# A per-subject residual matmul on one core: where the store is issued, how two engines share the copies, and a new start-up

## The chip, the cores and the metric

One core of one Trainium2 chip runs the kernel. The metric is the device time of one execution in microseconds (us). Three runs of the kernel before gave 332.45, 332.52 and 333.44 us; the median is 332.52 us.

## What is computed

```python
# x (128, 128, 1024) f32, itok_B_0_7 (128,) int32 in 0..7, L0_cond_weights (8, 128, 128) f32
w = weights[subjects]                       # one 128x128 matrix for each of the 128 samples
out = jnp.einsum('bct,bcd->bdt', x, w)
return x + out
```

Each of the 128 samples is 128 channels by 1024 time steps in f32 (512 KB). It is read once and written once: 67 MB in, 67 MB out.

## The kernel before

The residual is folded into the weights: `add_eye` adds the identity to each of the eight matrices, so that a product with `w + 1` is already the output.

**Tiles and pairs.** A tile is two samples (`a` = 0, 1), each on one half of the partitions: channel `h*2 + r` of sample `a` lies on partition `a*64 + h`, in row `r`. There are 64 tiles. Two tiles make a pair (four samples, 2 MB), and there are 32 pairs; loads and stores move a whole pair. `x_ring` has 10 slots (5 pairs), `results` has places for 6 pairs, and `product` in PSUM is double buffered by tile (`PRODUCTS = 2`).

**Engines.** Each one runs a program written out by hand, and semaphores alone set the order between them:

- SP (`sync`) loads the weights and then pair after pair (L108). For the first lap it issues four loads at once, and the fifth when pair 0 has landed. A later load waits for `picked` (L105), that is until POOL has filled the weight slots of the same pair.
- POOL builds the identity. Then, for each sample, it copies the subject's matrix from `weight_bank` to `weight_ring` (L136), four copies a pair. From pair 5 on it waits until the pair that held the slots has been multiplied.
- The weight bank itself is a reordered copy of the weights in four quarters, made by the helper `bank`: two quarters on DVE (L149), two on ACT (L180). POOL waits for all four.
- PE multiplies a tile in 8 matmuls (L217), which the trace records as 16, when the copies of the tile two before are out of PSUM (`dve_copied`, `act_copied`, one initial count of `PRODUCTS` each) and, at a pair's first tile, when the pair has landed (`x_in`). Before the first tile it waits for `picked` to reach 2.
- ACT and DVE copy the product out of PSUM into `results`. A tile has 8 blocks of 32 x 1024; `ACT_BLOCKS` says how many of them, from the front, ACT takes, and DVE takes the rest:

```python
BLOCKS = [(a, q) for a in range(2) for q in range(Q)]
ACT_BLOCKS = (4, 5)
for a, q in BLOCKS[:ACT_BLOCKS[tile % 2]]:
    last = act.copy(target(tile, a, q), rows(tile, a, q))
```

- ACT also issues the store of each pair (L202), behind its last copy of the pair's second tile, once both `act_copied` and `dve_copied` count that tile. Before the first copy into a place of `results` both engines wait for the store of six pairs earlier (`pair_out`).

Of the kernel before, what the change touches and what calls it, by code (L numbers as in the profile page):

```python
# [5 lines left out]
PSUM_BANK_COLS = 512  # L6
DMA_INC = 16
SLOTS = 10
PAIR = 2
LOADS_AHEAD = 4  # L10
PRODUCTS = 2
RESULTS = 6


def subject_residual_kernel(nc, x, subjects, weights, out):
# [12 lines left out]
    S, _, D = weights.shape  # L28
# [6 lines left out]
    PAIRS, PAIR_SLOTS = TILES // PAIR, SLOTS // PAIR  # L35
# [3 lines left out]
    SUBJECT_ROWS = 16  # L39

    BLOCKS = [(a, q) for a in range(2) for q in range(Q)]
    ACT_BLOCKS = (4, 5)

    LOW, HIGH = slice(0, H), slice(H, C)
    EVENS, ODDS = slice(0, S, 2), slice(1, S, 2)
# [3 lines left out]
    out_of_pair = out.rearrange("(n g) (k q) t -> n (g k) (q t)", g=PAIR * 2, q=Q)  # L49

    with ExitStack() as ctx:
        x_ring = ctx.enter_context(nc.sbuf_tensor("x_ring", [C, SLOTS, R, T], f32))
        results = ctx.enter_context(nc.sbuf_tensor("results", [C, RESULTS, Q, T], f32))
# [8 lines left out]
        product = [[ctx.enter_context(nc.psum_tensor(f"product{i}_{a}", [D, T], f32)) for a in range(2)]  # L62
                   for i in range(PRODUCTS)]

        subjects_in = ctx.enter_context(nc.semaphore("subjects_in"))
        clamped = ctx.enter_context(nc.semaphore("clamped"))
        weights_in = ctx.enter_context(nc.semaphore("weights_in"))
# [4 lines left out]
        bank_high = ctx.enter_context(nc.semaphore("bank_high"))  # L72
# [14 lines left out]
        def target(tile, a, q):  # L87

            pair, j = divmod(tile, PAIR)
            g = j * 2 + a  # L90
            return results[g * K:(g + 1) * K, pair % RESULTS, q, :]

        def rows(tile, a, q):

            return product[tile % PRODUCTS][a][q * K:(q + 1) * K, :]
# [14 lines left out]
        @block.gpsimd  # L110
        def _(pool):
            def subjects_of(pair):

                _, numbers = nc.values_load_multi_w_load_instructions(  # L114
                    subject_row[0:1, pair * PAIR * 2:(pair + 2) * PAIR * 2], engines=(mybir.EngineType.Pool,), min_val=0,
                    max_val=S - 1, skip_runtime_bounds_check_because="DVE has clamped subject_row to 0 .. S - 1")
                return numbers

            pool.memset(eye[:, :], 0.0).then_inc(eye_zero, 1)  # L119
            pool.wait_ge(eye_zero, 1)  # L120
            for half in (LOW, HIGH):
                pool.affine_select(eye[half, :], eye[half, :], pattern=[[-1, H]], base=0, channel_multiplier=1,  # L122
                                   compare_op=mybir.AluOpType.not_equal, fill=1.0).then_inc(eye_made, 1)
            pool.wait_ge(clamped, 1)
            for pair in range(PAIRS):
                if pair % 2 == 0:
                    numbers = subjects_of(pair)
                if pair == 0:
                    pool.wait_ge(bank_low, 1)
                    pool.wait_ge(bank_high, 1)  # L130
                elif pair >= PAIR_SLOTS:
                    pool.wait_ge(multiplied, (pair - PAIR_SLOTS + 1) * PAIR)
                for j in range(PAIR):
                    slot = pair * PAIR % SLOTS + j
                    for a, half in enumerate((LOW, HIGH)):
                        done = pool.tensor_copy(weight_ring[half, slot, :, :],  # L136
                                                weight_bank[half, bass.ds(numbers[(pair % 2 * PAIR + j) * 2 + a], 1), :, :])
                    done.then_inc(picked, 1)

        @block.vector  # L140
        def _(dve):
            def add_eye(r):
                cells = weight_halves[:, :, r, slice(r, D, R)]
                return dve.tensor_tensor(cells, cells, eye[:, :].rearrange("h (s k) -> h s k", s=1).broadcast_to(  # L144
                    (C, S // 2, H)), add)

            def bank(half, source, subjects_of):

                return dve.tensor_copy(  # L149
                    weight_bank[half, subjects_of, :, :].rearrange("h i r (q k) -> h i r q k", q=Q),  # L150
                    weight_halves[source, :, :, :].rearrange("h i r (k q) -> h i r q k", q=Q))

            dve.sem_inc(dve_copied, PRODUCTS)
            dve.wait_ge(subjects_in, DMA_INC)
            dve.tensor_scalar(subject_row[0:1, :], subject_row[0:1, :], 0, S - 1, mybir.AluOpType.max,  # L155
                              mybir.AluOpType.min).then_inc(clamped, 1)
            dve.wait_ge(weights_in, DMA_INC)
            dve.wait_ge(eye_made, 2)
            add_eye(0)
            add_eye(1).then_inc(eyes_added, 1)  # L160
            dve.wait_ge(eyes_added, 1)
            bank(LOW, LOW, EVENS)
            bank(LOW, HIGH, ODDS).then_inc(bank_low, 1)
            for tile in range(TILES):
                pair = tile // PAIR
                dve.wait_ge(multiplied, tile + 1)
                if tile % PAIR == 0 and pair >= RESULTS:
                    dve.wait_ge(pair_out[pair % RESULTS], pair // RESULTS * DMA_INC)
                if tile + PRODUCTS < SLOTS:


                    dve.wait_ge(picked, tile + (PRODUCTS + 1))
                for a, q in BLOCKS[ACT_BLOCKS[tile % 2]:]:
                    last = dve.tensor_copy(target(tile, a, q), rows(tile, a, q))  # L174
                last.then_inc(dve_copied, 1)

        @block.scalar
        def _(act):
            def bank(half, source, subjects_of):
                return act.copy(  # L180
                    weight_bank[half, subjects_of, :, :].rearrange("h i r (q k) -> h i r q k", q=Q),
                    weight_halves[source, :, :, :].rearrange("h i r (k q) -> h i r q k", q=Q))

            act.dma_start(subject_row[:, :], subjects.rearrange("(one b) -> one b", one=1).broadcast_to(
                (SUBJECT_ROWS, B))).then_inc(subjects_in, DMA_INC)
            act.sem_inc(act_copied, PRODUCTS)
            act.wait_ge(eyes_added, 1)
            bank(HIGH, LOW, EVENS)
            bank(HIGH, HIGH, ODDS).then_inc(bank_high, 1)
            for tile in range(TILES):  # L190
                pair, j = divmod(tile, PAIR)
                place = pair % RESULTS
                act.wait_ge(multiplied, tile + 1)
                if j == 0 and pair >= RESULTS:
                    act.wait_ge(pair_out[place], pair // RESULTS * DMA_INC)  # L195
                for a, q in BLOCKS[:ACT_BLOCKS[tile % 2]]:
                    last = act.copy(target(tile, a, q), rows(tile, a, q))  # L197
                last.then_inc(act_copied, 1)
                if j == PAIR - 1:
                    act.wait_ge(act_copied, tile + (PRODUCTS + 1))  # L200
                    act.wait_ge(dve_copied, tile + (PRODUCTS + 1))
                    act.dma_start(out_of_pair[pair], results[:, place, :, :]).then_inc(pair_out[place], DMA_INC)  # L202
            for place in range(RESULTS):
                act.wait_ge(pair_out[place], DMA_INC * len(range(place, PAIRS, RESULTS)))

        @block.tensor
        def _(pe):
            def multiply(tile, slot, landed):
                pe.wait_ge(dve_copied, tile + 1)
                pe.wait_ge(act_copied, tile + 1)  # L210
                if slot % PAIR == 0:
                    pe.wait_ge(x_in[slot // PAIR], landed)
                for n in range(BANKS):
                    cols = slice(n * PSUM_BANK_COLS, (n + 1) * PSUM_BANK_COLS)
                    for r in range(R):
                        for a, half in enumerate((LOW, HIGH)):
                            last = pe.matmul(product[slot % PRODUCTS][a][:, cols], weight_ring[half, slot, r, :],  # L217
                                             x_ring[half, slot, r, cols], start=r == 0, stop=r == R - 1,
                                             tile_position=(a * H, 0))
                last.then_inc(multiplied, 1)  # L220

            pe.wait_ge(picked, PRODUCTS)
            with pe.Fori(0, LAPS) as lap:
                for slot in range(SLOTS):
                    multiply(lap * SLOTS + slot, slot, lap * DMA_INC + DMA_INC)
            for slot in range(REST):
                multiply(LAPS * SLOTS + slot, slot, DMA_INC * (LAPS + 1))
# [14 lines left out]
```

## Time and profile before

| What | Value |
|---|---|
| Median of three runs | 332.52 us |
| The profiled execution's own time | 333.19 us |
| Its span, first to last instruction | 331.4 us |
| ACT busy | 294.2 us, 89% |
| DVE busy | 276.7 us, 84% |
| PE busy | 238.9 us, 72% |
| Moved by DMA | 134.84 MB, mean 407 GB/s over the span |

The span is what the rows of the trace add up to. The profiled execution took 1.8 us more than its span, and 0.7 us more than the median of the three runs. A difference of 0.3% (1.0 us) is about what a measurement of this kernel can tell from no change. PE, PEld (weight loads), DVE, ACT and POOL are the engines; SPq and ACTq are the queues on which SP and ACT issue transfers.

### The profile page before, as it was taken

To read this page: it belongs to the slowest core of one execution; us is meant where nothing else is said; L and a number is where in the kernel's file an instruction comes from. 1 tells how busy PE (TensorE), PEld (TensorE's weight loads), DVE (VectorE), ACT (ScalarE), POOL (GpSimd) and SP (SyncE) were. 2 spreads that over 40 slices of the span, in tenths; PEclk is the share of its full clock that TensorE was granted. 3 is DMA by queue.
4 is the path that set the end of the run, shared out by engine and by line. 5 is a ranking of instruction groups with operands and counts; after the bars stand their busy time and mean duration, and the time that the engine had idled before them with its cause. 6 is when DMAs were issued, how large, how long until landed. Compare 5 with 4: busy or idle time off the path is not lost.

```text
span 331.4 us, 3183 instructions
## 1 busy us (share of the span) xinstructions
PE 238.9 (72%) x1024; PEld 106.1 (32%) x1024; DVE 276.7 (84%) x229; ACT 294.2 (89%) x291; POOL 51.9 (16%) x135
## 2 busy tenths in 40 slices
PE   0588787788778777877777787778778877877740
PEld 0233333334333333433343333333333433333320
DVE  3089998889988888898888889888888988888890
ACT  4189999999999999999999999999999999999991
POOL 0641011111110111111011111101111110000000
PEclk9999999999999999999999999999999999999995
DMA  7999999999999999999999999999999999996565
GB/s 285 423 421 430 424 422 430 436 427 422 435 428 434 419 428 431 430 429 437 414 428 431 440 419 435 417 441 414 431 436 420 430 433 421 439 422 279 221 255 253
DMA packets 13881, 134.84 MB, mean 407 GB/s; under 512 B 1056, under 2 KB 1584, under 8 KB 1584
## 3 DMA queue, kind: packets, MB, share of 16 engines
q1 hardware_dynamic: 9232, 67.64, 48.7%
q10 hardware_dynamic: 4640, 67.12, 47.4%
q8 instruction: 2, 0.03, 0.1%
q14 instruction: 7, 0.06, 0.0%
HBM read 67.64 MB, written 67.11 MB: 407 GB/s over the span
## 4 chain that ended last, share of the span: by engine, by line
ACT 80%; issue 11%; ACTq 3%; PE 2%; DMA 1%; POOLq 0%; DVE 0%; POOL 0%
ACT results L197 79%; ACTq L202 3%; PE product L217 2%; DMA weight_halves<-weights 1%; ACT weight_bank L180 1%; DVE weight_halves L144 0%; POOL weight_ring L136 0%; ACTq L195 0%; POOLq L114 0%; POOLq L136 0%; POOLq L130 0%
## 5 line engine op out<-in xcount | busy, mean ns | idle before, releaser
L197 ACT COPY results<-product 32x1024 f32<-32x1024 f32 x288 | 288.9, 1003 | 25.8 <-ACT results L197 14.2
L174 DVE COPY results<-product 32x1024 f32<-32x1024 f32 x224 | 273.7, 1222 | 41.0 <-PE product L217 28.2
L217 PE MATMUL product<-x_ring,weight_ring 64*128 64x512 f32 x1024 | 238.9, 605 | 80.0 <-ACT results L197 47.1
L217 PEld LDWEIGHTS product<-x_ring,weight_ring 64*128 64x128 f32 x1024 | 106.1, 188 | 211.9 <-issue 169.1
L136 POOL COPY weight_ring<-weight_bank 64x256 f32 x128 | 51.1, 399 | 220.0 <-PE product L217 206.9
L180 ACT COPY weight_bank<-weight_halves 64x1024 f32<-64x1024 f32 x2 | 4.0, 1996 | 3.3 <-DVE weight_halves L144 3.2
L155 DVE TENSOR_SCALAR subject_row<-subject_row 1x128 int32<-1x128 int32 x1 | 0.2, 214 | 3.9 <-DMA subject_row<-subjects 3.9
L180 ACT ACT_TABLE_LOAD x1 | 1.3, 1283 | 1.3 <-PEq L234 1.3
L149 DVE COPY weight_bank<-weight_halves 64x1024 f32<-64x1024 f32 x2 | 2.1, 1060 | 0.0
L144 DVE TENSOR_TENSOR weight_halves<-weight_halves,eye 128x256 f32<-128x256 f32 x2 | 0.8, 424 | 0.9 <-DMA weight_halves<-weights 0.9
L122 POOL TENSOR_SCALAR_AFFINE_SELECT eye<-eye 64x64 f32<-64x64 f32 x2 | 0.5, 236 | 0.3 <-POOL eye L119 0.2
L119 POOL MEMSET eye<- 128x64 f32 x1 | 0.2, 152 | 0.3 <-POOLq L234 0.3
L234 POOL MEMSET const-float32-0.0<- 128x1 f32 x1 | 0.1, 99 | 0.2 <-issue 0.2
L234 POOL MEMSET const-float32-1.0<- 128x1 f32 x1 | 0.1, 99 | 0.0
L234 POOL MEMSET const-bfloat16-1.0<- 128x1 bf16 x1 | 0.1, 99 | 0.0
L234 POOL MEMSET const-uint8-127<- 128x1 uint8 x1 | 0.1, 99 | 0.0
## 6 DMA issues: line engine op xcount, KB each, us to landing
x_ring<-x SPq DMA_DIRECT2D x32, 2048.0 KB, 24.3
out<-results ACTq DMA_DIRECT2D x32, 2048.0 KB, 11.7
weight_halves<-weights SPq DMA_DIRECT2D x1, 512.0 KB, 4.3
subject_row<-subjects ACTq DMA_DIRECT2D x1, 8.0 KB, 3.2
```

Of the source, the lines that this page charges most:

```text
L119: pool.memset(eye[:, :], 0.0).then_inc(eye_zero, 1)
L122: pool.affine_select(eye[half, :], eye[half, :], pattern=[[-1, H]], base=0, channel_multiplier=1, compare_op=mybir.AluOpType.not_equal, fi ...
L136: done = pool.tensor_copy(weight_ring[half, slot, :, :], weight_bank[half, bass.ds(numbers[(pair % 2 * PAIR + j) * 2 + a], 1), :, :])
L144: return dve.tensor_tensor(cells, cells, eye[:, :].rearrange("h (s k) -> h s k", s=1).broadcast_to((C, S // 2, H)), add)
L149: return dve.tensor_copy(weight_bank[half, subjects_of, :, :].rearrange("h i r (q k) -> h i r q k", q=Q), weight_halves[source, :, :, :].r ...
L155: dve.tensor_scalar(subject_row[0:1, :], subject_row[0:1, :], 0, S - 1, mybir.AluOpType.max, mybir.AluOpType.min).then_inc(clamped, 1)
L174: last = dve.tensor_copy(target(tile, a, q), rows(tile, a, q))
L180: return act.copy(weight_bank[half, subjects_of, :, :].rearrange("h i r (q k) -> h i r q k", q=Q), weight_halves[source, :, :, :].rearrang ...
L197: last = act.copy(target(tile, a, q), rows(tile, a, q))
L202: act.dma_start(out_of_pair[pair], results[:, place, :, :]).then_inc(pair_out[place], DMA_INC)
L217: last = pe.matmul(product[slot % PRODUCTS][a][:, cols], weight_ring[half, slot, r, :], x_ring[half, slot, r, cols], start=r == 0, stop=r ...
L234: nc = bacc.Bacc("TRN2", target_bir_lowering=False, num_devices=1)
```

## The change

Four things change.

1. **The store.** ACT issues the store of pair p-1 behind its first copy of pair p, and the last one at the end. The waits for `act_copied` and `dve_copied` go with it.
2. **The shares.** `ACT_BLOCKS` becomes (4, 4, 5, 4, 5), a mean of 4.4 blocks of 8. Over 64 tiles ACT makes 281 copies where it made 288, DVE 231 where it made 224.
3. **Zeros on TensorE.** DVE writes zeros into 512 columns of the last place of `results`. PE multiplies them six times into `product[1][0]` before its first tile. PE then waits for `picked` 1 where it waited for 2; that tile 1 has its weights is now ensured by `dve_copied`, whose second initial count DVE gives after `picked` 2.
4. **The bank.** DVE makes three of the four quarters, ACT one. `bank_high` counts to 2.

```diff
+WARM_UP = 6
-    ACT_BLOCKS = (4, 5)
+    ACT_BLOCKS = (4, 4, 5, 4, 5)
...
-                    pool.wait_ge(bank_high, 1)
+                    pool.wait_ge(bank_high, 2)
...
+            dve.memset(results[:, RESULTS - 1, 0, 0:PSUM_BANK_COLS], 0.0).then_inc(zeroed, 1)
+
+            dve.sem_inc(dve_copied, 1)
...
             bank(LOW, HIGH, ODDS).then_inc(bank_low, 1)
+            bank(HIGH, LOW, EVENS).then_inc(bank_high, 1)
+            dve.wait_ge(picked, PRODUCTS)
+            dve.sem_inc(dve_copied, PRODUCTS - 1)
...
+            def store(pair):
+                place = pair % RESULTS
+                act.wait_ge(act_copied, (pair + 1) * PAIR + PRODUCTS)
+                act.wait_ge(dve_copied, (pair + 1) * PAIR + PRODUCTS)
+                act.dma_start(out_of_pair[pair], results[:, place, :, :]).then_inc(pair_out[place], DMA_INC)
...
-            bank(HIGH, LOW, EVENS)
             bank(HIGH, HIGH, ODDS).then_inc(bank_high, 1)
...
-                for a, q in BLOCKS[:ACT_BLOCKS[tile % 2]]:
+                blocks = BLOCKS[:ACT_BLOCKS[tile % len(ACT_BLOCKS)]]
+                act.copy(target(tile, *blocks[0]), rows(tile, *blocks[0]))
+                if j == 0 and pair:
+
+                    store(pair - 1)
+                for a, q in blocks[1:]:
                     last = act.copy(target(tile, a, q), rows(tile, a, q))
                 last.then_inc(act_copied, 1)
-                if j == PAIR - 1:
-                    act.wait_ge(act_copied, tile + (PRODUCTS + 1))
-                    act.wait_ge(dve_copied, tile + (PRODUCTS + 1))
-                    act.dma_start(out_of_pair[pair], results[:, place, :, :]).then_inc(pair_out[place], DMA_INC)
+            store(PAIRS - 1)
...
-            pe.wait_ge(picked, PRODUCTS)
+
+            pe.wait_ge(zeroed, 1)
+            zeros = results[:, RESULTS - 1, 0, 0:PSUM_BANK_COLS]
+            for _ in range(WARM_UP):
+                pe.matmul(product[PRODUCTS - 1][0][:, 0:PSUM_BANK_COLS], zeros[:, 0:D], zeros, start=True, stop=True)
+            pe.wait_ge(picked, 1)
```

The place of the store in ACT's program, at pairs 0 and 1. `results<-product_0` and `results<-product_1` are the copies of samples a = 0 and a = 1; a copy that waits for `multiplied` begins a tile. Before:

```order
L197 COPY results<-product_0 32x1024 [waits multiplied]
L197 COPY results<-product_0 32x1024 x3
L197 COPY results<-product_0 32x1024 [waits multiplied]
L197 COPY results<-product_0 32x1024 x3
L197 COPY results<-product_1 32x1024
L202 DMA out<-results 128x4096 [waits dve_copied,act_copied]
```

And after the change:

```order
L209 COPY results<-product_0 32x1024 [waits multiplied]
L214 COPY results<-product_0 32x1024 x3
L209 COPY results<-product_0 32x1024 [waits multiplied]
L214 COPY results<-product_0 32x1024 x3
L209 COPY results<-product_0 32x1024 [waits multiplied]
L195 DMA out<-results 128x4096 [waits dve_copied,act_copied]
L214 COPY results<-product_0 32x1024 x3
```

The store of pair 0 has moved behind the first copy of tile 2, and with it behind that copy's wait for `multiplied`.

The start of DVE's program, from the clamping of the subject numbers to the first copies out of PSUM, is this in the changed kernel:

```order
L155 MEMSET results 128x512
L159 TENSOR_SCALAR subject_row<-subject_row 1x128 [waits subjects_in]
L146 TENSOR_TENSOR weight_halves<-weight_halves,eye 128x4x64 [waits eye_made,weights_in]
L146 TENSOR_TENSOR weight_halves<-weight_halves,eye 128x4x64
L151 COPY weight_bank<-weight_halves 64x4x256 [waits eyes_added]
L151 COPY weight_bank<-weight_halves 64x4x256 x2
L181 COPY results<-product_1 32x1024 [waits picked,multiplied]
```

The memset stands first, and there are three `bank` copies where there were two.

## Rows read from the trace of the kernel before

**Rows 1.** The page: part 1 (busy) and part 4 (chain that ended last).

```profile
PE 238.9 (72%) x1024; PEld 106.1 (32%) x1024; DVE 276.7 (84%) x229; ACT 294.2 (89%) x291; POOL 51.9 (16%) x135
...
ACT 80%; issue 11%; ACTq 3%; PE 2%; DMA 1%; POOLq 0%; DVE 0%; POOL 0%
```

**Rows 2.** Timeline 200 to 212 us, one pair: start, length, engine, what, [idle before].

```profile
199.82 0.34 ACTq L202 DMA_DIRECT2D out<-results  x1
199.93 3.70 PE L217 MATMUL product<-x_ring,weight_ring 64*128 64x512 f32 x16 [1.42 <-ACT results L197]
200.25 9.13 ACT L197 COPY results<-product 32x1024 f32<-32x1024 f32 x9 [0.47 <-ACT results L197]
203.67 3.70 DVE L174 COPY results<-product 32x1024 f32<-32x1024 f32 x3 [0.21 <-PE product L217]
208.29 4.92 DVE L174 COPY results<-product 32x1024 f32<-32x1024 f32 x4 [0.91 <-PE product L217]
209.42 0.34 ACTq L202 DMA_DIRECT2D out<-results  x1
```

**Rows 3.** Stretches: length, busy and count of each engine, clock, DMA share, GB/s.

```profile
0.00:20.00 20.00, 7.75 (x26) 3.44 (x28) 4.99 (x7) 7.17 (x5) 8.80 (x27) 1.00 0.91 366
20.00:60.00 40.00, 31.11 (x136) 13.48 (x132) 37.41 (x32) 37.88 (x39) 6.46 (x17) 1.00 1.01 427
...
260.00:300.00 40.00, 30.87 (x134) 13.56 (x130) 35.74 (x30) 37.70 (x38) 3.19 (x8) 1.00 1.01 430
300.00:310.00 10.00, 7.41 (x32) 3.36 (x33) 8.95 (x8) 9.40 (x11) 0.00 (x0) 1.00 0.70 297
310.00:320.00 10.00, 7.41 (x32) 3.31 (x32) 8.95 (x8) 9.43 (x10) 0.00 (x0) 1.00 0.53 221
```

**Rows 4.** Pair loads by stretch: those issued at 23.4, 52.1 (last of four), 272.8 us.

```profile
DMA to landing us min/median/max: 16.2/16.2/16.2
...
DMA to landing us min/median/max: 16.2/19.1/20.1
...
DMA to landing us min/median/max: 32.4/32.4/32.4
```

**Rows 5.** DMA, 0 to 305.2 us: all packets, then load queue (q1) and store queue (q10).

```profile
DMA packets 13446, 128.52 MB, mean 421 GB/s; under 512 B 1007, under 2 KB 1535, under 8 KB 1535
...
q1 hardware_dynamic: 9232, 67.64, 52.9%
q10 hardware_dynamic: 4206, 60.81, 46.6%
```

**Rows 6.** DMA, 32 to 37 us (a store beside loads), then 15 to 25 us (loads alone).

```profile
q10 hardware_dynamic: 85, 1.39, 64.9%
q1 hardware_dynamic: 83, 0.68, 32.1%
...
q1 hardware_dynamic: 548, 4.23, 101.4%
```

**Rows 7.** All stores, then the last one alone (issued at 324.6 us).

```profile
DMA to landing us min/median/max: 6.3/11.7/12.8
...
DMA to landing us min/median/max: 6.3/6.3/6.3
```

**Rows 8.** Timeline of the start.

```profile
3.94 0.21 DVE L155 TENSOR_SCALAR subject_row<-subject_row 1x128 int32<-1x128 int32 x1 [3.94 <-DMA subject_row<-subjects]
5.83 4.00 ACT L180 COPY weight_bank<-weight_halves 64x1024 f32<-64x1024 f32 x2 [3.24 <-DVE weight_halves L144]
5.83 2.13 DVE L149 COPY weight_bank<-weight_halves 64x1024 f32<-64x1024 f32 x2
10.08 8.91 POOL L136 COPY weight_ring<-weight_bank 64x256 f32 x20 [8.41 <-ACT weight_bank L180]
12.25 9.23 PE L217 MATMUL product<-x_ring,weight_ring 64*128 64x512 f32 x32 [12.25 <-POOL weight_ring L136]
18.09 9.13 ACT L197 COPY results<-product 32x1024 f32<-32x1024 f32 x9 [8.26 <-PE product L217]
```

**Rows 9.** Timeline of ACT at the end.

```profile
315.02 0.34 ACTq L202 DMA_DIRECT2D out<-results  x1
315.45 9.13 ACT L197 COPY results<-product 32x1024 f32<-32x1024 f32 x9 [0.47 <-ACT results L197]
324.62 0.34 ACTq L202 DMA_DIRECT2D out<-results  x1
```

**Rows 10.** Two stretches after the last matmul, columns as in rows 3.

```profile
318.80:325.00 6.20, 0.04 (x1) 0.00 (x0) 3.67 (x3) 5.72 (x6) 0.00 (x0) 0.90 0.32 137
325.00:331.40 6.40, 0.00 (x0) 0.00 (x0) 0.00 (x0) 0.00 (x0) 0.00 (x0) 0.50 0.77 328
```

More of the change, by code:

```diff
@@ L63, in subject_residual_kernel @@
                    for i in range(PRODUCTS)]
+        zeroed = ctx.enter_context(nc.semaphore("zeroed"))
         subjects_in = ctx.enter_context(nc.semaphore("subjects_in"))
@@ L151, in bank @@
                     weight_halves[source, :, :, :].rearrange("h i r (k q) -> h i r q k", q=Q))
-            dve.sem_inc(dve_copied, PRODUCTS)
+            dve.memset(results[:, RESULTS - 1, 0, 0:PSUM_BANK_COLS], 0.0).then_inc(zeroed, 1)
+            dve.sem_inc(dve_copied, 1)
             dve.wait_ge(subjects_in, DMA_INC)
@@ L172, in _ @@
                     dve.wait_ge(picked, tile + (PRODUCTS + 1))
-                for a, q in BLOCKS[ACT_BLOCKS[tile % 2]:]:
+                for a, q in BLOCKS[ACT_BLOCKS[tile % len(ACT_BLOCKS)]:]:
                     last = dve.tensor_copy(target(tile, a, q), rows(tile, a, q))
```

## The prediction

> **What bounds the kernel now.** I read the busy line and the chain first. ACT is the busiest engine and holds 80% of the chain that ended last [rows 1]. The timeline of one pair shows how: the store is issued at 199.82 us and again at 209.42 us, so a pair takes 9.60 us, and ACT fills it with nine copies in 9.13 us and one idle 0.47 us [rows 2]. That idle time is the store: ACT waits for its own last copy, issues, and only then begins the next tile. DVE has seven copies of 1.23 us in the same time, PE two tiles of 3.70 us each. So the kernel looks like one bound by ACT.
>
> The stretches say that a second limit stands right behind it. From 20 to 300 us the DMA share is 1.01, at 427 to 430 GB/s [rows 3]. A pair is one load and one store of 2.097 MB, 4.194 MB in all, and at 428 GB/s that takes 9.80 us, which is longer than ACT's 9.60 us. The kernel gets away with it because loads start five pairs ahead, and it lives off that lead. The time from a load's issue to its landing shows the lead being used up: 16.2 us for the load issued at 23.4 us, 20.1 us for the one at 52.1 us, 32.4 us for the last, issued at 272.8 us [rows 4]. That last load lands at 272.8 + 32.4 = 305.2 us. Its pair is multiplied just before ACT can start on it: ACT's nine copies begin at 315.45 us, the store of the pair before goes out at 315.02 us [rows 9], and PE starts about 0.1 us behind that issue as in [rows 2], so at 315.1 us. The data waited 9.9 us. The run ends before the lead does.
>
> **The change part by part.**
>
> *Shares and store on ACT.* ACT now has 8.8 copies a pair on average. At 9.13/9 = 1.014 us [rows 2] they take 8.93 us. The issue of the store (0.34 us) stands behind the first copy of the next pair, so it runs while that copy of 1.0 us does, and the 0.47 us go away, if DVE is done by then. DVE has 7.2 copies of 1.23 us, 8.86 us. The two engines need nearly the same, so I do not take 8.93 us but the loop through one PSUM buffer: multiply 3.70, then the longer of five ACT copies (5.07) and four DVE copies (4.92), and 0.3 us of semaphores, 9.1 us for two tiles. If the store's wait for DVE is not covered by the one copy, the 0.47 us come back, at most: 8.93 + 0.47 = 9.4 us. So computing takes 9.1 us a pair, between 8.9 and 9.4.
>
> *The start.* A quarter of the bank takes DVE 1.06 us and ACT 2.00 us [rows 8]. Three on DVE end at 5.83 + 3.2 = 9.0 us, one on ACT at 7.8 us; before, ACT ended at 9.83 us. POOL starts 0.8 us sooner, and PE waits for two of its copies (0.45 us each) where it waited for four, 0.9 us more. PE starts at about 10.4 us instead of 12.25 us; the first pair landed at 10.0 us, so that no longer leaves room. The first tile took 18.09 - 12.25 = 5.84 us, a later one 3.70 us: the zeros should give the 2.1 us back, because it begins at full speed. In all 4.0 us on the first copy, which then begins at 14.1 us. The trace has no such matmul over 128 rows. Two half-height ones of 512 columns side by side take 3.70/4 = 0.93 us at full speed, and double at half; six are 5.6 to 11.1 us. Started at about 2 us they end between 7.6 and 13 us, so at worst 2.7 us of the gain is lost. The memset has no row on DVE either: nothing to 1.1 us (the cost of a bank quarter, which is larger), before 3.94 us where DVE is idle anyway [rows 8]. I take nothing. DVE's new wait for `picked` 2 ends at about 11.4 us, before there is a tile to copy.
>
> *What computing alone would give.* First copy at 14.1 us, 32 pairs of 9.1 us to 305.3 us, then 6.3 us until the last store has landed [rows 7] and 0.5 us to the end of the span: a span of 312.1 us, 19.3 us less than 331.4 us.
>
> *What the transfers allow.* Computing at 9.1 us a pair would need 4.194/9.1 = 461 GB/s, and no stretch shows over 430 [rows 3]. Where both queues have work, the store queue moved 1.39 MB in 5 us and the load queue 0.68 MB [rows 6]: a store takes two thirds, 278 GB/s, and is done in 7.5 us, however many loads wait. So stores keep pace with computing, and the loads pay: at a store every 9.1 us they have 428 - 230 = 198 GB/s and take 10.6 us each. The lead shrinks by 1.5 us a pair. The load issued at 52.1 us (pair 8) landed at 72.2 us [rows 4]; the changed kernel would multiply that pair at 10.4 + 8 x 9.1 = 83 us. A lead of 11 us lasts for 7 pairs. **From about pair 15, near 150 us, PE waits for x**, and the pace is that of the transfers, 9.8 us a pair.
>
> Then only the total of bytes counts, and the faster start is worth nothing: the queues were full from 4 us on before as well. When the last load had landed, at 305.2 us, 128.52 MB had been moved: 67.64 MB by the load queue and 60.81 MB, or 29.0 stores, by the other [rows 5]. In the changed kernel the store of pair 29 is issued behind the first copy of pair 30, so 3.7 + 1.2 = 4.9 us after pair 30 has landed, and pair 31 lands 9.8 us after pair 30. Of these stores 11.7 us pass to landing [rows 7], 7.5 of them data, some 3.3 us ahead of the data. So the store is 1.6 us into its data when pair 31 lands: 29.2 stores. That is 0.2 x 2.097 = 0.4 MB more, 1.0 us. **Pair 31 lands at 306.2 us.**
>
> *The tail.* From there: multiply 3.8 us (0.1 us of semaphore with it); ACT's nine copies (tiles 62 and 63 fall on 5 and 4) 9.13 us and 0.1 us; DVE, with seven, is done sooner, and the second tile's matmuls end at 7.5 us, before ACT needs them; issue and landing of the last store 6.3 us [rows 7]; 0.5 us to the end. Sum 19.9 us, and the span is 326.1 us, 5.3 us below 331.4 us. Before, this stretch took 331.4 - 305.2 = 26.2 us, since the lead of 9.9 us stood in it. So the gain is that lead, less a multiply and the later stores. With the 1.8 us outside the span this is 327.9 us for the profiled execution; the median of the runs lies 0.7 us lower, **327.2 us**.
>
> The DMA rate carries this sum. The Trainium skill ("DMA: Bandwidth & Descriptors", Specifications) gives the HBM limit of a core as about 358 GB/s: by it 134.84 MB would take 377 us, which the trace contradicts with 427 to 430 GB/s over 280 us. The same section's fabric ceiling of 435 GB/s would, as an estimate from that page, bring the landing of pair 31 down by 4.6 us (286 us times the ratio of the rates) and the time to 322.6 us.
>
> *Bounds*, as times of a run like the 327.2 us. If only 28.5 stores precede the last load, it lands 3.4 us sooner (0.7 x 2.097/0.428): 323.8 us. If all thirty of pairs 0 to 29 do, it lands 3.9 us later: 331.1 us. If the mean rate from 20 us on is 423 GB/s, as with loads alone [rows 6], instead of 428, the landing moves by 3.4 us: 330.6 us.
>
> **Rivals.**
>
> *Nothing to be measured.* The last pair lands later than I think, at 310 us or more, because all stores up to pair 29 come first, or because a pair counts as landed only when the slowest share of it has. In the stretch 300 to 310 us the share of the DMA is still 0.70, not lower [rows 3], which hints at stragglers behind 305 us. Then 331.1 to 333 us, and it decides from a landing at 310.5 us (331.5 us) on. For it speaks that a starved ring waits for every straggler, where a lead hides them; against it that the load with the straggler is what the 305.2 us already include.
>
> *Slower: TensorE's clock.* In the trace the clock is 1.00 (2.4 GHz) through all the pauses of 1.4 us and less [rows 2, 3]; after the last matmul, near 318.8 us, it falls, and from 325 us it is 0.50 (1.2 GHz) [rows 10]. The changed kernel leaves a pause of 9.8 - 7.4 = 2.4 us in each starved pair, a length that no row shows in one piece beside matmuls. One slow start costs 2.1 us (5.84 - 3.70), and 7.4 + 2.1 = 9.5 us still fits in 9.8 us. It decides once PE needs more than 9.8 us a pair, so from 2.4 us of loss, one tile and a bit at half speed. With both tiles starting slow, 11.6 us a pair; over 17 starved pairs that is up to 31 us, but PE would then hardly pause and be back at full speed, so I price half of the pairs, 15 us on top of 327.2 us: about 342 us. The Trainium skill ("TensorE: Matmul & The Clock Gate", Why this matters for your kernels) warns that pauses between bursts send TensorE back to half clock; by that rule the pauses made here are a risk, and the trace shows the fall only behind the last matmul.
>
> *Transfers do not bind.* They keep up with 9.1 us a pair after all: 332.5 - 19.3 = 313.2 us. No stretch above 430 GB/s supports it.
>
> *The store is not hidden* (9.4 us a pair): by computing alone a span of 14.1 + 32 x 9.4 + 6.8 = 321.7 us, still under the 326.1 us of the transfers. So whether the first two parts do all they say hardly shows in the time.
>
> **Chances.** My forecast, bound by transfers with the last landing between 303 and 310 us: 0.73. No measurable difference (331.5 to 333.5 us): 0.14. Slower by the clock: 0.09. Computing alone: 0.04. Faster is the first and the last, 0.77. The likeliest case reaches from 323.8 to 331.1 us, and with the larger part of the second I give 324.0 to 332.2 us, which leaves out under 0.2.
>
> **What would show it.** In the profile after: the DMA share stays at 1.0 up to about 305 us; loads take up to nearly 50 us to land (five deep at 9.8 us); PE's idle time is ended by the landing of x_ring in the second half, and no longer by ACT; stores are issued 9.1 us apart early and 9.8 us apart late; the first copy begins near 14 us; ACT is busy 287 us and DVE 285 us. The forecast is wrong if stores stay 9.1 us apart to the end, if the clock in the middle is below 1.00, or if the last load lands after 311 us.

## The result and the profile after

The changed kernel takes 331.2 us (median of 20 runs, 328.86 to 333.62), the kernel before 332.72 us in as many runs beside it. The ratio is 0.9944 with a 95% interval of 0.9925 to 0.9963: a gain of 0.4 to 0.75%, or 1.5 us. The forecast was 327.2 us, a gain of 5.3 us or 1.6%. The direction is right and the size is not: under a third of the forecast gain came. The runs of the changed kernel also spread over 4.8 us, those of the kernel before over 1.4 us. The profiled execution took 329.79 us with a span of 328.0 us, so it is one of the faster ones.

From the page of the changed kernel, busy times and the chain that ended last:

```profile
PE 250.2 (76%) x1036; PEld 107.7 (33%) x1036; DVE 286.9 (87%) x238; ACT 285.0 (87%) x283; POOL 51.5 (16%) x135
...
DMA 49%; ACT 19%; PE 12%; DVE 9%; issue 4%; POOL 2%; POOLq 1%; ACTq 1%
```

ACT lost 9 us of work and DVE gained 10, as the shares say. The chain, which was 80% ACT [rows 1], is now half DMA: PE waits for x. Stretches of the changed kernel, with the columns of rows 3:

```profile
60.00:100.00 40.00, 33.34 (x144) 14.39 (x144) 39.28 (x33) 39.26 (x40) 6.33 (x16) 1.00 1.01 430
100.00:140.00 40.00, 29.34 (x130) 13.46 (x132) 37.09 (x32) 37.41 (x39) 7.91 (x20) 0.99 1.01 428
...
220.00:260.00 40.00, 32.01 (x130) 13.70 (x128) 34.46 (x29) 34.93 (x36) 6.33 (x16) 0.91 1.01 429
```

From 60 to 100 us ACT and DVE are busy 98% of the time. Later they are not, and in some stretches the clock is below 1.00, which it never was in rows 3 while PE had matmuls left. The DMA columns read as before: 1.01 and 428 to 430 GB/s.

PE's waits in the changed kernel's second half (100 to 320 us): us in total, times, longest; then four of the eight places where it waited for a pair:

```profile
PE product L231 <- DMA x_ring<-x: 22.0, 8, 4.8
...
120.23 7.14 PE L231 MATMUL product<-x_ring,weight_ring 64*128 64x512 f32 x32 [2.37 <-DMA x_ring<-x]
...
181.06 8.51 PE L231 MATMUL product<-x_ring,weight_ring 64*128 64x512 f32 x32 [4.84 <-DMA x_ring<-x]
...
278.13 8.83 PE L231 MATMUL product<-x_ring,weight_ring 64*128 64x512 f32 x32 [2.33 <-DMA x_ring<-x]
308.36 7.14 PE L231 MATMUL product<-x_ring,weight_ring 64*128 64x512 f32 x32 [2.67 <-DMA x_ring<-x]
```

The first wait is at 120 us. The first three waits are 9.76 us apart, as the forecast had it; from then on they are not spread evenly over the pairs. In all there are eight lumps of up to 4.8 us, with up to four pairs in a row between them that PE does not wait for at all. Behind four of the lumps the two next tiles take 8.5 to 10.0 us (a slow start), behind the other four 7.14 to 7.45 us (full clock, or nearly).

The start and the end of ACT and PE in the changed kernel:

```profile
1.46 7.85 PE L240 MATMUL product<-results 128*128 128x512 f32 x12 [1.46 <-DVE results L155]
10.62 7.14 PE L231 MATMUL product<-x_ring,weight_ring 64*128 64x512 f32 x32 [1.32 <-POOL weight_ring L138]
14.37 1.00 ACT L209 COPY results<-product 32x1024 f32<-32x1024 f32 x1 [6.52 <-PE product L231]
...
312.11 1.00 ACT L209 COPY results<-product 32x1024 f32<-32x1024 f32 x1 [2.12 <-PE product L231]
...
321.26 0.34 ACTq L195 DMA_DIRECT2D out<-results  x1
```

The zeros end at 9.3 us, PE starts at 10.62 us where it started at 12.25 us [rows 8], and the first copy is at 14.37 us, 3.7 us sooner. The last store is issued at 321.26 us, 3.4 us sooner than in rows 9.

What the DMA had moved in the changed kernel when pair 31 landed, at 308.2 us, and then what it moved from 302 us to that landing:

```profile
DMA packets 13580, 130.52 MB, mean 423 GB/s; under 512 B 1019, under 2 KB 1547, under 8 KB 1547
...
q10 hardware_dynamic: 4340, 62.81, 47.7%
...
q10 hardware_dynamic: 157, 2.13, 81.1%
q1 hardware_dynamic: 29, 0.20, 7.5%
```

62.81 MB are 29.95 stores, where 29.0 stood in front of the last landing in rows 5. The last two lines show why the landing is so late: in the last 6.2 us the load queue moved only 0.20 MB, a tenth of a load. A pair has landed when the last of the sixteen counts on its semaphore has come. For pair 31 the trace has the first at 301.0 us, eleven by 302.2 us, and the last at 308.2 us. From pair 12 on, the landings (last counts) are 6.8 to 12.3 us apart, 9.9 us on average.

### The profile page after: what moved, and what is told of

It reads as the page before. It is cut to its first block, busy times and chain, and to the rows that moved or that the text cites. A ratio compares the mean times of both kernels' runs of the same rounds, so it can differ in the third digit from the quotient of the medians.

```text
span 328.0 us, 3209 instructions
## 1 busy us (share of the span) xinstructions
PE 250.2 (76%) x1036; PEld 107.7 (33%) x1036; DVE 286.9 (87%) x238; ACT 285.0 (87%) x283; POOL 51.5 (16%) x135
## 4 chain that ended last, share of the span: by engine, by line
DMA 49%; ACT 19%; PE 12%; DVE 9%; issue 4%; POOL 2%; POOLq 1%; ACTq 1%
DMA x_ring<-x 48%; ACT results L214 16%; PE product L231 12%; DVE results L181 8%; ACT results L209 3%; POOL weight_ring L138 2%; DMA weight_halves<-weights 1%; DVE weight_bank L151 1%; POOLq L116 1%; ACTq L195 1%; POOLq L138 0%; DVE weight_halves L146 0%; POOLq L52 0%; ACTq L194 0%; POOLq L132 0%
## 5 line engine op out<-in xcount | busy, mean ns | idle before, releaser
L181 DVE COPY results<-product 32x1024 f32<-32x1024 f32 x231 | 282.2, 1222 | 29.4 <-PE product L231 24.0
L231 PE MATMUL product<-x_ring,weight_ring 64*128 64x512 f32 x1024 | 242.4, 616 | 63.8 <-DVE results L181 25.8
L214 ACT COPY results<-product 32x1024 f32<-32x1024 f32 x217 | 217.6, 1003 | 5.0 <-DVE results L181 2.1
L231 PEld LDWEIGHTS product<-x_ring,weight_ring 64*128 64x128 f32 x1024 | 104.5, 192 | 201.7 <-issue 142.6
L209 ACT COPY results<-product 32x1024 f32<-32x1024 f32 x64 | 64.0, 1000 | 26.7 <-PE product L231 25.5
L240 PE MATMUL product<-results 128*128 128x512 f32 x12 | 7.8, 822 | 1.5 <-DVE results L155 1.5
L240 PEld LDWEIGHTS product<-results 128*128 128x128 f32 x12 | 3.1, 271 | 5.3 <-issue 3.9
L187 ACT COPY weight_bank<-weight_halves 64x1024 f32<-64x1024 f32 x1 | 2.0, 2031 | 3.2 <-DVE weight_halves L146 3.2
L151 DVE COPY weight_bank<-weight_halves 64x1024 f32<-64x1024 f32 x3 | 3.2, 1075 | 0.1
## 6 DMA issues: line engine op xcount, KB each, us to landing
x_ring<-x SPq DMA_DIRECT2D x32, 2048.0 KB, 36.7
```

Source lines behind the costliest of these rows:

```text
L151: return dve.tensor_copy(weight_bank[half, subjects_of, :, :].rearrange("h i r (q k) -> h i r q k", q=Q), weight_halves[source, :, :, :].r ...
L187: return act.copy(weight_bank[half, subjects_of, :, :].rearrange("h i r (q k) -> h i r q k", q=Q), weight_halves[source, :, :, :].rearrang ...
L209: act.copy(target(tile, *blocks[0]), rows(tile, *blocks[0]))
L240: pe.matmul(product[PRODUCTS - 1][0][:, 0:PSUM_BANK_COLS], zeros[:, 0:D], zeros, start=True, stop=True)
```

## The experiments

Each group of kernels ran on one chip, beside runs of the kernel before there. Chips differ by some tenths of a us, so the ratio to the kernel before is what can be compared across groups.

### One part undone at a time

`store_old` moves the store back behind the pair's last copy:

```diff
-                if j == 0 and pair:
-                    store(pair - 1)
...
                 last.then_inc(act_copied, 1)
+                if j == PAIR - 1:
+                    store(pair)
```

> The changed kernel with the store issued again behind ACT's last copy of the pair. Theory (transfers bind the changed kernel, and its end is the landing of pair 31 plus some 20 us): computing alone takes 8.93 + 0.47 = 9.4 us a pair, which still outruns the 9.8 us of the transfers, so the time stays within 1 us of the changed kernel's (331.2 us). Stores then go out some 2 us sooner in a starved pair, which puts up to 0.2 store more in front of the last load: +1 us at most. Rival (ACT still binds, and moving the store is what gained): 0.47 x 31 = 14 us slower at most, near 333 us or more.

`shares_old`:

```diff
-    ACT_BLOCKS = (4, 4, 5, 4, 5)
+    ACT_BLOCKS = (4, 5)
```

> The changed kernel with the old shares (4, 5) for ACT. Theory: ACT needs nine copies, 9.13 us a pair, with the store hidden, under 9.8 us, so the time stays within 1 us of 331.2 us. Rival (the shares carry the gain): 0.2 us a pair, 6 us slower, which would be slower than the kernel before.

`start_old` takes back the zeros and the third bank copy on DVE, and PE waits for `picked` 2:

```diff
-            dve.memset(results[:, RESULTS - 1, 0, 0:PSUM_BANK_COLS], 0.0).then_inc(zeroed, 1)
...
-            bank(HIGH, LOW, EVENS).then_inc(bank_high, 1)
...
+            bank(HIGH, LOW, EVENS)
             bank(HIGH, HIGH, ODDS).then_inc(bank_high, 1)
...
-            for _ in range(WARM_UP):
-                pe.matmul(product[PRODUCTS - 1][0][:, 0:PSUM_BANK_COLS], zeros[:, 0:D], zeros, start=True, stop=True)
-            pe.wait_ge(picked, 1)
+            pe.wait_ge(picked, PRODUCTS)
```

> The changed kernel with the start of the kernel before: no zeros on TensorE, two bank quarters on ACT, PE waits for four of POOL's copies. Theory: the DMA queues are full from 4 us on either way, so 4 us of later start only move the point at which the lead is used up, and the time stays within 1 us of 331.2 us. Rival (the start counts in full): 4 us slower, 335 us.

Measured: 329.71, 330.99 and 330.01 us, ratios 0.9912 (0.9887 to 0.9938), 0.9931 (0.9907 to 0.9954) and 0.9906 (0.9881 to 0.993). None is slower than the changed kernel (0.9944), so no single part is needed for the gain; the rivals of 6, 4 and several us fall.

The three traces do not say the same, however. In `shares_old` and `start_old` PE waits seven and five times for x, as in the changed kernel. In `store_old` it never does. PE's waits in it, and then two of its rows:

```profile
PE product L229 <- issue: 23.2, 13, 2.1
PE product L229 <- ACT results L211: 22.2, 24, 1.4
PE product L229 <- DVE results L181: 16.8, 20, 1.6
...
126.14 8.83 PE L229 MATMUL product<-x_ring,weight_ring 64*128 64x512 f32 x32 [1.93 <-issue]
...
174.42 3.70 PE L229 MATMUL product<-x_ring,weight_ring 64*128 64x512 f32 x16 [1.93 <-issue]
```

From pair 12 on every pair has landed 1.9 us or more before PE takes it up. So in `store_old` the transfers set nothing: computing holds the pace to the end. Its stores are 9.63 us apart on average from 24.12 to 322.52 us. Where the clock stays full, five pairs take 47.3 us, or 9.46 us a pair, close to the 9.4 us expected. But five times PE starts slowly behind a pause of 1.9 to 2.1 us (two tiles in 8.83 us, as at 126.14 us), and each time the next store comes 1.0 us later. That the old place of the store costs nothing is thus a near tie: computing at 9.63 us a pair ends at 329.3 us, about where the transfers let the changed kernel end (328.0 and 329.8 us in two traces). It does not show that the store's place is worth nothing to computing. `after_light` below computes a pair in 8.97 us.

### One part alone

`shares_only` is the kernel before with the new shares and nothing else:

```diff
-    ACT_BLOCKS = (4, 5)
+    ACT_BLOCKS = (4, 4, 5, 4, 5)
```

> The kernel before with the new shares (4, 4, 5, 4, 5) and nothing else. Computing takes 8.8 x 1.014 + 0.47 = 9.4 us a pair. Theory (9.4 us outruns the transfers' 9.8 us, so this alone brings the whole gain): within 1 us of the changed kernel, near 330 to 331 us. Rival (each part brings its share of the gain): near 332 us, not to be told from the kernel before.

Measured: 332.17 us, ratio 1.0002 (0.9984 to 1.0021). The expectation was wrong: this part alone brings nothing that can be measured. By the forecast's own sums the kernel is at 18.1 + 32 x 9.4 + 6.8 = 325.7 us by computing and about 326 us by transfers. Its trace, with a span of 330.1 us, says which of the two was off:

```profile
PE product L217 <- ACT results L197: 23.6, 26, 1.4
PE product L217 <- issue: 22.9, 13, 1.9
PE product L217 <- DVE results L174: 16.2, 20, 1.6
```

PE never waits for x here either. Pair 31 lands at 306.8 us, 2.7 us before PE takes it up. So no late landing delays this kernel; computing alone holds it. Its stores are 9.545 us apart on average. With the clock full a pair takes 9.46 us, and three slow starts behind pauses of 1.92 us (80.11, 175.61 and 271.10 us) add 1.0 us each: 18.1 + 32 x 9.545 + 6.8 = 330.3 us. The forecast had no term for slow starts in a kernel that computing holds. ACT's waits stand in the trace as expected, 21 times behind its own last copy, for the issue of the store, and 7 times for DVE. With either of the other two parts beside it (`start_old`, `store_old`) the gain is there.

### What each kernel does when transfers do not bind

In `after_light` and `before_light` each store writes only the first half of its columns; the other half of `out` is not written, so a pair moves 3.1 MB instead of 4.2 MB.

```diff
-                act.dma_start(out_of_pair[pair], results[:, place, :, :]).then_inc(pair_out[place], DMA_INC)
+                act.dma_start(out_of_pair[pair][:, 0:Q * T // 2], results[:, place, 0:Q // 2, :]).then_inc(pair_out[place], DMA_INC)
```

> The changed kernel, but each store writes only the first half of its columns (the other half of out is left unwritten), so a pair moves 3.1 MB where it moved 4.2 MB and the transfers need 7.3 us a pair. Theory: PE never waits for x after the start, stores go out every 9.1 us to the end, and the span is near 14.4 + 32 x 9.1 + 0.1 + 4 + 0.5 = 310 us, 18 us less than the 328.0 us of the changed kernel. Rival (computing is what holds the changed kernel at 9.6 to 9.8 us a pair late in the run): within 3 us of 328 us.

> The kernel before, but each store writes only the first half of its columns (the other half of out is left unwritten). Theory (ACT bounds the kernel before at 9.60 us a pair and no pair is ever waited for): the pace stays at 9.60 us, only the last store gets shorter, by 1.0 MB or 2.4 us: span near 329 us against 306.8 us of the changed kernel with the same light stores, so the change takes 22 us off computing alone. Rival (transfers already held the kernel before back): span well under 325 us.

Measured: `after_light` 308.69 us (span 306.8 us), `before_light` 330.78 us (span 329.0 us). The light changed kernel from 60 to 260 us, then PE's waits in it over the whole run:

```profile
60.00:260.00 200.00, 165.39 (x716) 71.23 (x718) 195.95 (x161) 196.29 (x197) 34.82 (x88) 1.00 0.98 350
```

```profile
PE product L231 <- DVE results L181: 27.7, 38, 1.6
PE product L231 <- ACT results L214: 14.7, 18, 1.3
PE product L231 <- issue: 7.7, 6, 1.3
```

Two rows of the timeline of `before_light`:

```profile
199.91 0.34 ACTq L202 DMA_DIRECT2D out<-results  x1
...
209.51 0.34 ACTq L202 DMA_DIRECT2D out<-results  x1
```

The pair of runs settles the main reading. The kernel before keeps 9.60 us a pair with a quarter of its bytes gone, so ACT bounded it. The changed kernel never waits for x then, its stores are 8.97 us apart on average, its clock stays at 1.00, and it is 22.2 us shorter, as the change to the computing says (19.3 us forecast). With all the bytes it keeps 3.4 us of these 22 in the profiled executions and 1.5 us in the medians. The DMA share is still 0.98 in the light kernel, at 350 GB/s, though every later pair lands some 22 us before it is used: a share near 1 does not by itself tell that transfers bind, the waits do.

### What sets the end

`after_again` is the changed kernel itself.

> The changed kernel once more, unaltered, on the chip and in the rounds of the three kernels beside it, and for a second profile of it. Theory (its end is set by the last time PE waits for x: from that landing on, the remaining pairs follow at 9.1 us each, plus up to 1.7 us where the pause had brought TensorE to half its clock, and 6.3 us for the last store; the landings depend on the slowest of a load's sixteen shares, which differs from run to run): its runs lie between 328.5 and 333.5 us again, and in the profile that sum gives the end within 0.5 us, whatever pair the last wait falls on. Rival (the landing of pair 31 alone sets the end): end = that landing + 19.8 us.

Measured: 330.52 us (329.65 to 331.59, 6 runs), ratio 0.9931 (0.9916 to 0.9947). The profiled execution took 331.59 us, with a span of 329.8 us. PE, ACT and ACTq at its end, from the last wait for x on:

```profile
298.88 8.83 PE L231 MATMUL product<-x_ring,weight_ring 64*128 64x512 f32 x32 [2.97 <-DMA x_ring<-x]
304.31 1.00 ACT L209 COPY results<-product 32x1024 f32<-32x1024 f32 x1 [3.10 <-PE product L231]
304.38 0.34 ACTq L195 DMA_DIRECT2D out<-results  x1
...
314.25 3.70 PE L231 MATMUL product<-x_ring,weight_ring 64*128 64x512 f32 x16 [1.26 <-DVE results L181]
314.28 0.34 ACTq L195 DMA_DIRECT2D out<-results  x1
...
323.02 0.34 ACTq L195 DMA_DIRECT2D out<-results  x1
```

Here the last wait is for pair 30, which landed at 298.7 us. Pair 31 landed at 306.7 us and PE did not look for it before 309 us. From 298.88 us there are 5.43 us to the first copy, then two pairs to the last issue at 323.02 us (18.7 us where the sum says 18.2), 6.3 us to landing and 0.5 us: 329.8 us. By the rival, the landing of pair 31 plus 19.8 us, it would have been 326.5 us. The 5.43 us are also 1.68 us more than the 3.75 us (308.36 to 312.11) behind the last wait of the other profile. The stretches around it say why, the second being the pause, the third the restart:

```profile
290.00:295.80 5.80, 5.04 (x24) 2.07 (x20) 5.60 (x6) 5.72 (x7) 0.00 (x0) 1.00 1.04 442
295.90:298.80 2.90, 0.01 (x1) 0.00 (x0) 2.85 (x3) 2.85 (x4) 0.00 (x0) 1.00 0.96 410
298.80:301.80 3.00, 2.92 (x10) 1.59 (x12) 1.31 (x2) 2.39 (x3) 0.00 (x0) 0.72 0.95 407
301.80:307.80 6.00, 5.91 (x24) 2.60 (x20) 3.46 (x3) 3.45 (x4) 0.00 (x0) 0.86 0.72 302
```

After a pause of 2.97 us the granted clock fell, to a mean of 0.72 (between 2.4 and 1.2 GHz) just when the matmuls came back. The profile of `start_old` ends in the same way one pair earlier: last wait at 288.51 us for pair 29, matmuls of 8.83 us, three pairs at 9.1 us on average, span 328.1 us, though pair 31 landed at 306.3 us. In that of `shares_old` the last wait is for pair 28, at 279.27 us, with four pairs at 9.15 us behind it: span 328.1 us, pair 31 at 306.3 us too.

### Stores held back, loads cut in two

If too many stores stand in front of the last loads, they can wait: after the last landing there is computing enough to hide them. `hold16`:

```diff
+HOLD_FROM = 16
...
-                if j == 0 and pair:
+                if j == 0 and 0 < pair <= HOLD_FROM:
                     store(pair - 1)
+                elif j == 0 and pair > HOLD_FROM + 1:
+                    store(pair - 2)
+                elif tile == TILES - 1:
+                    store(PAIRS - 2)
```

> The changed kernel, but from pair 17 on each store is issued one pair later (behind the first copy of pair p goes the store of pair p-2; that of pair 30 behind the first copy of tile 63). Theory (total transfers bind; what counts is how many stores stand in front of the last load, since after it some 13 us of computing hide 2.7 stores): one store less in front, 4.9 us off the last landings, up to 4.9 us off the end, of which the last stores, now closer together, take back up to 1 us: 326 to 328 us. Rival (stores are not in the loads' way, each load's landing is set by something else): no change, or slower by the later stores.

`hold24` is the same with `HOLD_FROM = 24`.

> As hold16, but the stores are held back by a pair only from pair 25 on. Theory (what counts is the number of stores in front of the last landings, not when the holding begins): the same as hold16, 326 to 328 us. Rival (the gain came from fewer pauses in the middle of the run): near the changed kernel, 330 to 331 us.

`tile_loads` is the changed kernel with one load, and one semaphore, for each tile:

```diff
-                sp.dma_start(x_ring[:, place * PAIR:(place + 1) * PAIR, :, :], x_of_pair[pair]).then_inc(x_in[place], DMA_INC)
+                for s in range(place * PAIR, (place + 1) * PAIR):
+                    sp.dma_start(x_ring[:, s:s + 1, :, :], x_of_pair[pair][:, s % PAIR:s % PAIR + 1, :]).then_inc(x_in[s], DMA_INC)
...
-                if slot % PAIR == 0:
-                    pe.wait_ge(x_in[slot // PAIR], landed)
+                pe.wait_ge(x_in[slot], landed)
```

> The changed kernel with each pair loaded as two tiles (1 MB each, a semaphore for each slot), so PE can start on a pair when its first half is there. Theory: where PE waits for x, it waits for half a load less, 2.5 to 3.7 us sooner, in the middle of the run this only shortens the pauses, since the transfers hold the pace; at the end it takes up to 3.7 us (one tile's multiply) off, and pauses get shorter, so that TensorE's clock stays at 1.00 more often: 327.5 to 330 us. Rival (64 smaller loads cost the queues more than they give): slower than the changed kernel.

`hold_tile` and `hold24_tile` have both edits.

> hold16 with each pair loaded as two tiles. Theory: loading by tiles shortens the last wait and its slow start by up to 2 us on top of hold16, 325 to 327 us. Rival (the smaller loads' slowest share lands as late as before): the same as hold16.

> hold_tile with the holding only from pair 25 on. Theory (only what stands in front of the last landings counts): the same as hold_tile, 325.5 to 327 us. Rival (holding over the second half also helps by fewer pauses once loads come by tiles): 1 us or more slower than hold_tile.

| Kernel | Median, us | Ratio to before (95%) |
|---|---|---|
| after_again | 330.52 | 0.9931 (0.9916 to 0.9947) |
| hold16 | 327.16 | 0.9837 (0.9801 to 0.9874) |
| tile_loads | 329.93 | 0.991 (0.9891 to 0.9929) |
| hold24 | 326.73 | 0.9821 (0.9794 to 0.9849) |
| hold_tile | 326.38 | 0.979 (0.9765 to 0.9816) |
| hold24_tile | 326.61 | 0.9812 (0.9784 to 0.9841) |

Holding the stores back gives another 3.4 us on the same chip (`hold16` against `after_again`), and where the holding begins makes no difference that these runs could tell (`hold24` ran on another chip, and its ratio overlaps with that of `hold16`). What `hold16` had moved when pair 31 landed in its trace, at 301.4 us, and its last stores:

```profile
q1 hardware_dynamic: 9232, 67.64, 53.6%
q10 hardware_dynamic: 4064, 58.73, 45.6%
```

```profile
294.85 9.43 PE L235 MATMUL product<-x_ring,weight_ring 64*128 64x512 f32 x32 [4.22 <-DMA x_ring<-x]
...
309.67 0.34 ACTq L196 DMA_DIRECT2D out<-results  x1
...
314.63 0.34 ACTq L196 DMA_DIRECT2D out<-results  x1
...
319.58 0.34 ACTq L196 DMA_DIRECT2D out<-results  x1
```

58.73 MB are 28.0 stores in front, 1.4 fewer than in `after_again` (61.58 MB, landing at 306.7 us), and the landing is 5.3 us sooner. The last wait for x is for pair 30 again, at 294.85 us against 298.88 us. Behind that wait the copies set the pace and not the transfers: the last issues are 4.95 us apart because one tile's copies stand between them, each of these stores lands 6.3 to 6.4 us after its issue, like the last one alone in rows 7, and the DMA share falls to 0.34 from 305 to 309 us. Whether a second store could be held back was not tried. In the trace of `hold24` the last wait for x is for pair 23, at 230.52 us. Pair 31 lands at 302.1 us with 28.5 stores in front, and the stores from 290.51 to 307.96 us are 8.7 us apart, so computing alone sets its end.

Loading by tiles is not told apart from the changed kernel by these runs (the intervals overlap), and with `hold16` it gives at most a little. PE then waits 15 times for 32.7 us in all instead of 9 times for 23.8 us: the smaller loads' last counts come as late as before. `hold_tile`, 2.1% below the kernel before (1.8 to 2.35%), is the best ratio measured; `hold24` on the same chip is simpler and overlaps with it, and `hold24_tile` is not told apart from either. The 2 us that `hold_tile` was to bring on top did not come.

## Why the prediction was right and where it failed

**Right.** ACT bounded the kernel before, and transfers bind the changed one; `before_light` and `after_light` show both. The median load takes 36.7 us to land where it took 24.3 us, PE waits for x from the middle of the run on (120 us; I had said 150), early stores are 9.0 us apart (81 us for the nine intervals from 24.34 us on), and the first copy came at 14.37 us (14.1 forecast). That the start is worth nothing in the presence of the other two parts is what `start_old` measured. By the fabric ceiling of 435 GB/s that the forecast took from the Trainium skill ("DMA: Bandwidth & Descriptors", Specifications) the end would have come earlier still; the stretches keep showing 427 to 431 GB/s, and the measurement decides.

**The step that failed** is "Then only the total of bytes counts", with the tail hung on it: that PE would be held at an even 9.8 us a pair, and that the landing of pair 31, with 29.2 stores in front, would set the end. The landing itself was well placed. It was forecast at 306.2 us; the traces have 308.2 us and 306.7 us for the changed kernel, and 306.3, 306.3 and 306.8 us for `start_old`, `shares_old` and `store_old`. The tail behind it was right to 0.1 us where pair 31 was the last that PE waited for (308.2 to 328.0 us, 19.8 us, against 19.9, whose terms add up to 19.8). But the landings are 6.8 to 12.3 us apart, not an even 9.8. A late one delays PE, and behind it the remaining pairs need 9.15 us each and get back 0.6 us a pair. So each of pairs 28 to 31 can be the one that decides, and the end is the latest of "landing of pair k, plus its slow start, plus the remaining pairs". It was pair 31 in the first trace, 30 in `after_again`, 29 in `start_old` and 28 in `shares_old`.

Part of the unevenness is that a pair counts as landed only with the slowest of its sixteen shares, one for each count. Pair 18 of the changed kernel, behind the longest wait, has its first count 9.8 us after that of pair 17, but its last 12.3 us after. It is not all of it: the first counts, too, are 5.0 to 11.6 us apart from pair 12 on, and what makes them so stays open.

I had named the slowest share under the rival "Nothing to be measured", with 0.14, and put its decision at a landing of pair 31 after 310.5 us. In three traces the end came late through pairs 28, 29 and 30 instead, with pair 31 on time. The bound for all thirty stores in front of the last load, 331.1 us, agrees with the measured 331.2 us by luck: in the first profile nearly all of them were in front (29.95), and the landing came at 308.2 us and not at the 310.1 us that goes with that bound.

**Two readings behind it.** The forecast said that the data of pair 31 waited 9.9 us in the kernel before. It waited 4.8 us: 315.1 us is where PE begins the pair's second tile, and its first begins at 310.00 us. The sum of the tail does not use the 9.9 us and stands without it. And the lead of 11 us at pair 8 took the landing of the kernel before, 72.2 us. In the changed kernel that pair lands at 78.6 us and PE takes it up at 82.96 us, so the lead is 4.4 us. At the forecast's 1.5 us a pair that lasts for three pairs, and the first of the waits is indeed for pair 12, at 120 us and not at 150 us.

**The sizes.** From the forecast to the profiled execution it is 1.9 us (327.9 against 329.8 us), all in the landing of pair 31, which had 29.95 stores in front of it instead of 29.2 (3.7 us by the bytes; 1.7 us of it came back because the mean rate from 20 us to the landing was 427.5 GB/s where it had been 425.0). In `after_again` it is 329.8 - 326.1 = 3.7 us of span, of which 1.7 us are the slow start behind pair 30 and the rest is that pair's early claim on the end. To the median it is 4.0 us: the forecast put the median 0.7 us below the profiled execution, and it lay 1.4 us above. Nothing here says which pair decided in the unprofiled runs; that their spread (4.8 us) comes from the same unevenness is argued, not shown.

**TensorE's clock.** The rival of 342 us did not happen: the pairs behind a slow start are at full speed again, and one slow start costs 1.4 to 2.8 us on two tiles. But the mechanism is real. The granted clock of a profiled run fell from 0.988 to 0.962, and behind pauses of 2.3 to 4.8 us the two next tiles took 8.5 to 10 us instead of 7.14. In this the trace agrees with the rule of the Trainium skill ("TensorE: Matmul & The Clock Gate", Why this matters for your kernels) that pauses between bursts cost TensorE its full clock. As to which pauses do it, the traces do not follow the page: one of 1.93 us did in `store_old` (126.14 us), one of 3.65 us did not in `after_again` (230.19 us), and the measurement decides. In the changed kernel transfers hold the pace, and a slow start can be seen to cost time only behind the last wait; the forecast had no term for that in the tail. In `shares_only` and `store_old`, which computing holds, three and five slow starts cost 1.0 us each. The forecast put a computing pace of 9.4 us at 321.7 us of span, under the 326.1 us of the transfers; `store_old` has about that pace and a span of 329.3 us. No kernel was tried that keeps the clock up through the pauses, so what it costs in the median run stays open.

**The store's new place** made no difference to the time beside the other two parts, though computing takes 9.0 us a pair with it (`after_light`) and 9.6 us without it (`store_old`): the transfers take that gain away. What no part of the forecast had weighed is the other use of that place: `hold16` shows that the moment of a store matters for the loads that it delays.

## What to carry to other kernels

When the engine that bounds a kernel is relieved, compare its new pace with the transfers' pace before adding up the gain; here 22 us of computing were taken off, and 3.4 us of span and 1.5 us of the median went. If two limits come within 1 or 2% of each other, look in the trace which of them holds each variant: equal times here had different causes. Where transfers hold it, the end is set by the latest of several uneven landings, and slack is what absorbs them. And once transfers bind, look at the order in which bytes are moved at the end: stores that later computing can hide should not stand in front of the last loads.

## What the runs showed that I had not expected

- The sixteen counts of one 2 MB load come 7 us apart late in a run (301.0 to 308.2 us for pair 31 of the changed kernel, 297.8 to 305.2 us in the kernel before), and up to 8.7 us in `store_old`; those of the first four loads come within 0.8 us. In the kernel before, this spread was hidden by the lead.
- A pause of 2.37 us left the clock at full speed (120.23 us), one of 2.33 us did not (278.13 us). In `store_old` a pause of 1.93 us did not at 126.14 us and one as long did at 174.42 us: the length of the pause alone does not tell.
- The zeros on TensorE ran 7.85 us for twelve records, and the clock behind them was full: the first two tiles took 7.14 us together where they had taken 9.23 us.
- DVE's memset of 128 x 512 took 0.49 us, inside the bounds given.
